# A three-stage decoder layer on one core: context loaded batch by batch, shorter lags, four load buffers, and routes moved beside the first group's spreading

## What is computed

```python
# layer 1: causal linear attention, one 16-wide head repeated 16 times
qkv = x @ qkv_w.T + qkv_b;  q, k, v = split(qkv, 3)
wei = where(tril, einsum('btd,bsd->bts', q, k), 0)
x = layernorm(x + tile(wei @ v, 16) @ proj_w.T + proj_b)
# layer 2: each batch's 77 ctx rows are aligned to its 256 x rows by dynamic time warping
D = sqrt(max(|ctx|^2 + |x|^2 - 2 ctx.x, 0))            # 77 x 256 per batch
R[i, j] = D[i, j] + min(R[i-1, j], R[i, j-1], R[i-1, j-1])
path = backtrack(R);  x = layernorm(x + sum of ctx rows along the path)
# layer 3: product-key memory with 64*64 experts, batch norm over all 8192 rows ahead of the query
xn = batchnorm(x) * gamma + beta;  q = (xn @ w_q.T)    # 2 halves, 8 heads, 128 wide
scores, idx = top_k(q . keys, 8)                       # per half
sc, pk = top_k(scores0[:, None] + scores1[None, :], 8) # 8 of the 64 sums
h = sigmoid(sc) * gelu(x . down[indices])
x = layernorm(x + sum of h * up[indices])
```

## Time and profile before

| | |
|---|---|
| time, median of 3 executions | 2913.73 us |
| lowest and highest | 2905.39 and 2916.35 us |
| the profiled execution: its own time | 2907.08 us |
| its span | 2905.3 us |
| mean granted PE clock | 0.956 |
| PE busy | 2652.9 us (91%) |
| DVE, POOL, ACT busy | 76%, 30%, 26% |
| stage 1, to the first DVE instruction of stage 2 | 207.4 us |
| recursion and path of stage 2 | 207.4 to 383.7 us |
| batch loop of stage 2 | 383.7 to about 480 us |
| stage 3 | from about 485 us to the end |

### The profile page before, as it was taken

The page is one execution under the profiler, slowest core; times in us unless marked ns, Lnnn a source line. Parts: engine busy times, 40 slices in busy tenths (PEclk is TensorE's granted clock), DMA queues, the critical chain, the costliest instruction groups (busy, mean ns, idle before and its releaser), DMA issues.

```text
span 2905.3 us, 104629 instructions
## 1 busy us (share of the span) xinstructions
PE 2652.9 (91%) x43108; PEld 2293.1 (79%) x43108; DVE 2210.9 (76%) x7510; ACT 761.9 (26%) x1340; POOL 857.1 (30%) x670
## 2 busy tenths in 40 slices
PE   6961167799999999999999999999999999999996
PEld 5851145688888888888888888888888888888895
DVE  5668966877777777777777777777777778777744
ACT  4740055322222222222222222222222222222210
POOL 1330142233333333333333333333333333333332
PEclk9985589999999999999999999999999999999997
DMA  5550337400000000000000000000000000000000
GB/s 174 172 161 23 65 112 177 72 13 13 11 13 10 13 12 12 13 13 13 14 13 13 13 14 13 13 14 13 13 14 13 13 13 14 13 14 13 10 10 12
DMA packets 84630, 99.34 MB, mean 34 GB/s; under 512 B 6189, under 2 KB 74702, under 8 KB 84046
## 3 DMA queue, kind: packets, MB, share of 16 engines
q1 hardware_dynamic: 84190, 92.94, 11.5%
HBM read 65.13 MB, written 27.79 MB: 32 GB/s over the span
## 4 chain that ended last, share of the span: by engine, by line
PE 82%; issue 7%; DVE 1%; DMA 1%; ACT 1%; POOL 0%; POOLq 0%; DVEq 0%; SPq 0%; ACTq 0%
PE bank L1078 32%; PE bank L1112 31%; PE bank L1096 9%; PE bank L1049 8%; PE bank L767 1%; DMA x_again<-x_scratch 1%; PE bank L770 1%; PE bank L1064 1%; PE bank L1036 1%; DVE hot L1295 0%; ACT x_sb L727 0%; POOL best L664 0%; DMA x_scratch<-x_sb 0%; DVE shared L1307 0%; ACT L1197 0%
## 5 line engine op out<-in xcount | busy, mean ns | idle before, releaser
L1015 POOL TENSOR_TENSOR hot<-hot,valsT 128x512 f32<-128x512 f32 x512 | 733.0, 1451 | 1662.8 <-DVE hot L1295 1662.8
L1078 PE MATMUL bank<-x2T,shared 128*64 128x128 f32 x16384 | 951.4, 274 | 4.6 <-issue 3.1
L1078 PEld LDWEIGHTS bank<-x2T,shared 128*64 128x64 f32 x16384 | 889.8, 137 | 26.6 <-issue 11.9
L1295 DVE TENSOR_TENSOR hot<-places,valsT 128x1024 f32<-128x1024 f32 x512 | 647.6, 1305 | 0.2 <-issue 0.2
L1112 PE MATMUL bank<-up,shared 64*128 64x256 f32 x4096 | 449.4, 379 | 1.5 <-DVE shared L1307 1.5
L1112 PE MATMUL bank<-up,gelh 64*128 64x256 f32 x4096 | 446.4, 377 | 0.0
L1112 PEld LDWEIGHTS bank<-up,shared 64*128 64x128 f32 x4096 | 397.1, 188 | 58.9 <-issue 11.4
L1112 PEld LDWEIGHTS bank<-up,gelh 64*128 64x128 f32 x4096 | 395.2, 187 | 56.2 <-issue 11.5
L1096 PE MATMUL bank<-hot 64*64 64x64 f32 x16384 | 303.1, 224 | 30.9 <-POOL hot L1015 16.3
L1096 PEld LDWEIGHTS bank<-hot 64*64 64x64 f32 x16384 | 267.9, 137 | 79.7 <-issue 79.7
L1307 DVE TENSOR_TENSOR shared<-bank,shared 128x512 f32<-128x512 f32 x256 | 164.7, 685 | 176.8 <-PE bank L1096 176.4
(11 more groups left out here) (151 smaller groups left out, 2169.5 us busy)
## 6 DMA issues: line engine op xcount, KB each, us to landing
x_scratch<-x_sb SPq DMA_DIRECT2D x64, 256.0 KB, 2.1
xT_sb<-in_xT SPq DMA_DIRECT2D x32, 256.0 KB, 2.9
x_sb<-in_x SPq DMA_DIRECT2D x32, 256.0 KB, 3.0
x_again<-x_scratch SPq DMA_DIRECT2D x32, 256.0 KB, 2.8
x_tile<-x_scratch SPq DMA_DIRECT2D x32, 256.0 KB, 3.9
up<-in_table SPq DMA_DIRECT2D x2, 4096.0 KB, 37.0
yo<-x_scratch SPq DMA_DIRECT2D x32, 256.0 KB, 3.0
out_y<-yo SPq DMA_DIRECT2D x32, 256.0 KB, 2.0
```

Of the source, the lines that this page charges most:

```text
L1015: pool.tensor_tensor(lo, lo, valsT[:, par, 2, TQ * q:TQ * (q + 1), None].to_broadcast([P, TQ, NK]), ALU.mult).then_inc(gated_ready, 1)
L1078: mm = pe.matmul(ps_h[q % 2][half(c), i, :], dnT[:, k, lo // 2, half(lo % 2)], x2T[:, par, k, c, :], start=(k == 0), stop=(k == CC - 1))
L1295: dve.tensor_tensor(hot[:, q % SLOTS], places[:, None, None, :].to_broadcast([P, 2, TQ, NK]), valsT[:, par, 0:2, TQ * q:TQ * (q + 1), None ...
```

## The change

1. **Stage 1.** ctx is loaded one batch at a time (`load_ctx`, two transfers of 77 KB), with two buffers for its columns; `norms` takes one batch per step with another instruction. All lags are shorter, and the order of the lists is another: `dist` runs 4 steps behind `qkv`, was 7. SP's list is written out in full: `load_x` lag 1, `store_x1` 5, `store_dist` 7, and a new `load_cost` at lag 8, which brings each batch's distances back as `cost` as soon as they are stored. The first x transfer goes ahead of the weights, a small Sqrt is done before anything waits, the reduction of the projection is cut in two, and the start of PE needs only some of POOL's constants (`pads`).
2. **Stage 2.** The `cost` loads are gone from its start. DVE's recursion waits only for the first of POOL's fills. `x1_again` has four buffers: `load(b)` waits for `warp(b-4)`, and the store is at lag 6, was 3.
3. **Stage 3.** DVE does `hots` of group 0 ahead of `route(1, 0)`, and `route(1, 1)` after the step of group 0, followed by `route(2, 0)`, `hots` of group 1 and `route(2, 1)`; so in that step no `hots` of group 1. PE turns the values of group 0 after `hidden` 6, was 8, and those of group 1 inside `output(0)`. ACT's gates move with them.

The diff, cut to its core:

```diff
-            ctx_cols = sa("ctx_cols", [P, CC, NB, S2])
+            ctx_cols = sa("ctx_cols", [P, CC, 2, S2])
...
+                def load_ctx(b, par):
+                    if later(b, 2):
+                        sp.wait_ge(norm_seen, b - 1)
+                        sp.wait_ge(ctxm2_ready, b - 1)
+                    sp.dma_start(ctx_rows[:, b, :], ctx_rows_d[b]).then_inc(rows_in[par], 16)
+                    sp.dma_start(ctx_cols[:, :, par, :], ctx_cols_d[:, b].rearrange("(k p) s -> p k s", k=CC))\
+                        .then_inc(cols_in[par], 16)
...
+                def load_cost(b, par):
+                    sp.wait_ge(dist_out[par], dmas(b, par))
+                    sp.dma_start(cost[b:P:NB, :], dist_d[b].rearrange("(g f) -> g f", g=NG)).then_inc(cost_in[par], 16)
...
-                pipeline(sp, [(load_xT, 0), (load_x, 5), (store_x1, 7), (store_dist, 10)], 12)
...
+                for i in range(1, NB + 9):
+                    for stage, lag, first in ((load_xT, 0, 2), (load_x, 1, 0), (store_x1, 5, 0), (store_dist, 7, 0),
+                                              (load_cost, 8, 0), (load_ctx, 4, 0)):
+                        if first <= i - lag < NB:
+                            stage(i - lag, (i - lag) % 2)
...
-                pipeline(pe, [(head, 2), (qkv, 0), (wei, 1), (turn_v, 1), (attn, 3), (turn_x1, 6), (dist, 7)], 10)
+                pe.wait_ge(pads, 1)
+                pe.wait_ge(w_in, 16 * 6)
+                pipeline(pe, [(qkv, 0), (head, 1), (dist, 4), (wei, 0), (turn_v, 0), (attn, 1), (turn_x1, 2)], 6)
...
-                pipeline(act, [(root, 9), (head, 2), (qkv, 0), (wei_off, 1), (ctx_scale, 6), (x1_cols, 6), (std, 4)], 12)
+                pipeline(act, [(qk, 0), (std, 2), (v, 0), (head, 1), (wei_off, 0), (ctx_scale, 3), (root, 4), (x1_cols, 2)], 6)
...
-                pipeline(dve, [(residual, 4), (recip, 5), (dist, 8), (wei_diag, 1), (v, 1), (setup, 1), (settle, None),
-                               (norms, 4), (stats, 4), (scale, 5), (settle, None), (aggr, 4)], 10)
+                pipeline(dve, [(recip, 2), (dist, 4), (settle, None), (scale, 2), (wei_diag, 0), (v, 0), (setup, 0),
+                               (residual, 1), (norms, 3), (settle, None), (stats, 1), (settle, None), (aggr, 1)], 6)
...
-            x1_sb = sw("x1_again", [P, 2, NT, C])
+            x1_sb = sw("x1_again", [P, 4, NT, C])
...
-                for g in range(NG):
-                    sp.dma_start(cost[NB * g:NB * (g + 1), :], dist_d[:, RG * T * g:RG * T * (g + 1)])\
-                        .then_inc(cost_in[g], 16)
...
-                pipeline(sp, [(load, 0), (store, 3)], 6)
+                pipeline(sp, [(load, 0, 4), (store, 6)], 8, unroll=4)
...
                     for lo in range(NK):
+                        if lo == 20 and not later(g, 1):
+                            turn_vals(1)
...
-                    if q == 8:
+                    if q == 6:
                         turn_vals(0)
...
-                route(1, 0)
                 for q in range(SLOTS):
                     hots(0, 0, q)
-                route(1, 1)
+                route(1, 0)
...
-                    if within(g, 2):
+                    if not later(g, 1):
+                        route(1, 1)
+                        route(2, 0)
+                        for q in range(SLOTS):
+                            hots(1, 1, q)
+                        route(2, 1)
+                    elif within(g, 2):
                         route(g + 2, 0)
                         route(g + 2, 1)
```

More of the change, by code:

```diff
@@ L81, in decoder_layer @@
         dn = shared[:, DN:].rearrange("p (j c) -> p j c", c=C)
+        cost = shared[:, 0:RG * T]
         w_in = sem("w_in")
         wq_in = sem("wq_in")
-        ctx_in = [sem(f"ctx_in{i}") for i in range(NB // 8)]
+        rows_in = [sem(f"rows_in{i}") for i in range(2)]
+        cols_in = [sem(f"cols_in{i}") for i in range(2)]
+        norm_seen = sem("norm_seen")
+        pads = sem("pads")
         consts = sem("consts")
@@ L118, in decoder_layer @@
         dist_out = [sem(f"dist_out{i}") for i in range(2)]
-        cost_in = [sem(f"cost_in{g}") for g in range(NG)]
+        cost_in = [sem(f"cost_in{i}") for i in range(2)]
         table_init = sem("table_init")
@@ L128, in decoder_layer @@
         bounds_ready = sem("bounds_ready")
-        x1_in = [sem(f"x1_in{i}") for i in range(2)]
+        x1_in = [sem(f"x1_in{i}") for i in range(4)]
         short_ready = sem("short_ready")
@@ L319, in _ @@
                 pool.memset(wqkv[:, :, GAP + HS:2 * GAP], 0.0)
+                pool.memset(proj[:, :], 0.0)
+                pool.memset(eps_col[:, :], EPS)
+                pool.drain()
+                pool.nop().then_inc(pads, 1)
                 pool.memset(ones[:, :], 1.0)
@@ L363, in turn_v @@
                     pe.wait_ge(vT_ready, b + 1)
+                    if not later(b, 1):
+                        pe.wait_ge(consts, 1)
                     if later(b, 1):
@@ L454, in ctx_scale @@
                 def ctx_scale(b, par):
-                    if not later(b, 1):
-                        for part in ctx_in:
-                            act.wait_ge(part, 32)
+                    act.wait_ge(cols_in[par], dmas(b, par))
                     if later(b, 2):
@@ L618, in one, with load @@
                     return ap[bass.ds(b, 1)].rearrange("a p t c -> (a p) t c")
-                def load(b, par):
-                    if later(b, 2):
-                        sp.wait_ge(warp_mm, b - 1)
-                    sp.dma_start(x1_sb[:, par], one(x1b, b)).then_inc(x1_in[par], 16)
+                def load(b, lane):
+                    if later(b, 4):
+                        sp.wait_ge(warp_mm, b - 3)
+                    sp.dma_start(x1_sb[:, lane], one(x1b, b)).then_inc(x1_in[lane], 16)
                 def store(b, par):
@@ L966, in vals_of @@
             def vals_of(g):
-                return ps_vals0 if isinstance(g, int) and g == 0 else ps_vals
+                return ps_vals0 if isinstance(g, int) and g < 2 else ps_vals
             def within(g, n):
@@ L1102, in output @@
                     pe.wait_ge(coef_ready, NA * (g + 1))
-                    if within(g, 1):
+                    if within(g, 1) and later(g, 1):
                         pe.wait_ge(valsT_ready, g + 2)
@@ L1133, in first @@
                         coefs(g, n)
-                        if n == 5 and within(g, 1):
-                            turn_vals(g + 1)
+                        if n == 5:
+                            if within(g, 1) and later(g, 1):
+                                turn_vals(g + 1)
                             if within(g, 2):
@@ L1349, in step @@
                                 hots(g, par, q)
-                            elif within(g, 1):
+                            elif within(g, 1) and later(g, 1):
                                 hots(g + 1, 1 - par, q - NQ)
-                    if within(g, 2):
+                    if not later(g, 1):
+                        route(1, 1)
[4 more added lines that the diff above has]
+                    elif within(g, 2):
                         route(g + 2, 0)
```

77 lines of the change are left out of this document (36 added, 41 removed).

## The result

| | before | changed |
|---|---|---|
| time, median of 16 executions each | 2906.82 us | 2914.02 us |
| span of the profiled execution | 2905.3 us | 2912.4 us |
| mean granted PE clock | 0.956 | 0.958 |
| first instruction of the recursion, on DVE | 207.38 us | 228.95 us |
| first turning on PE in stage 3 | 486.23 us | 501.09 us |

The ratio of changed to before is 1.0021, with a 95% interval from 1.0013 to 1.0028: 0.2% slower, so within 0.5%, where I forecast 0.5% less and a range that ended at 2912. (One of the 16 executions of the kernel before took 4055 us; the ratio leaves it out.) Stage 2 gained what was forecast and stage 3 two thirds of it. Stage 1, which was to be 3 us shorter, is 21.6 us longer.

The account below looks back on a forecast made before the run. PE was taken to bound stage 1's middle and stage 3, a DVE chain stage 2's recursion. Stages gave -3 - 6 - 6 = -15 us, from 2913.7 to 2898.7, 0.5% less; range for 8 in 10: 2878 to 2912.

Parts of the forecast that it names:

- Stage 1, start: Start of stage 1: ctx transfers leave the path; `residual(0)` at about 19, `residual(4)` at 38, 20 us ahead of before.
- Stage 1, middle: Middle of stage 1: a loop from `residual` through the distance store and `dist` back makes a batch 5.7 us, not 4.98.
- L: Landing time of the distance store that `dist` waits for in stage 1, taken as 2.3 us.
- The loops behind it: Other stage 1 loops claimed shorter: DVE's step about 4.3 us, ACT's 4.7, PE's 4.98.
- that rival: Stage 1 middle: the store lands fast, L 1.7, batch 5.1, middle 15 us shorter, 2884 us in all; 25%.
- Stage 1, end: From `residual(30)` to the recursion: 18.5 us instead of 23.5, 5 less.
- Stage 2: Recursion loop: with four buffers the x1 load waits go, 2.6 us a batch for 2.81; 6 us less (3 to 8).
- Stage 3: Start of stage 3: `coefs(0, 1)` starts 13.1 us earlier, new holes take some back; 6 us less (3 to 8).
- The holes: Three new PE waits in stage 3: 3.3 us, 3.5 us, and 1.7 us from group 0's norm delaying two `hots`.
- the rival: New waits eat the later gains: stage 2 gives nothing, stage 3 3 us as holes lower PE's clock; 2908 us; 20%.
- slower: the store queues: Stage 1, `dist`'s wait: small transfers keep the queues busy, L 3.5, batch 6.9, 2929 us; 8%.

Follow-up runs that it names:

- e11: Changed kernel with x1 store, distance store and ctx load lags one less, and SP issuing the distance store first in its step: 2881.77 us, ratio 0.9910 to before.
- e4: Changed kernel without cost loads in SP's loop; four 640 KB transfers at the end of stage 1 instead: 2923.68 us, ratio 1.0062 to before.
- e12: Changed kernel with the distance store and ctx load lags one less (6 and 3), x1 store still at lag 5: 2887.91 us, ratio 0.9930 to before.
- e1: Changed kernel with only the distance store one step earlier on SP (lag 6 for 7): 2908.46 us, ratio 1.0006 to before.
- e10: Changed kernel with x1 store, distance store and ctx load lags one less, and DVE's `dist` behind `scale`: 2876.66 us, ratio 0.9896 to before.

## Why the prediction was wrong, point by point

**Stage 1, start: right but for 2.4 us.** `residual(0)` was forecast at about 19 and came at 19.60; `residual(4)` at 38 came at 40.41. 17.6 us ahead of before, not 20.

**Stage 1, middle: the mechanism was right, one term was mis-sized, and this is the step that failed.** The loop was drawn as it runs. Its sum was 3.39 + L, and L was taken as 2.3: "1.6 for the store alone ... and 0.7 for two large transfers ahead". Measured in the step shown, L is 2.91, and 2.8 in the median. The rest is 3.57 for 3.39: `dist` to `scale` is 0.73, not 0.55, since 0.25 us of idle lie between them (the row of `scale`). The batch is 6.48 in that step and 6.39 in the mean (3.57 + 2.82), not 5.7. `residual(5)` came at 46.94 where 43.3 was forecast, 2.4 of these 3.6 us from the start, and the 25 batches after it at 6.38 add 17.1: together the 20.7 us by which `residual(30)` (206.50) missed 185.8.

What was wrong in the 2.3: I added a small queueing term to a landing. The runs show what a landing of 80 KB is in this queue: it comes 0.2 us behind that of the last transfer ahead, and takes 1.7 where those have landed early enough, as in the kernel before. Issued 0.92 behind a load that lands in 2.9 and 0.51 behind an x1 store that lands in 3.1, it takes 3.1 - 0.51 + 0.2 = 2.8. And the x1 store itself had gone from 2.1 to 3.1 where it stands 0.41 behind a load; with one more transfer ahead (e11) it takes 3.8.

The Trainium skill (DMA: Bandwidth & Descriptors, Queues, rings and completion order) has this as its rule: a semaphore increment lands only after the earlier writes of the same DMA engine. I cited it, but applied it to the x load alone, which gave a bound of 2.1; applied to the x1 store as well, with the 3.1 that this store has in the changed kernel, it gives 2.6. The runs agree with the rule: none of the 165 stores lands ahead of a transfer issued before it, L follows the ctx columns in e11, and in e4 taking away transfers issued behind the store leaves L alone.

**The loops behind it: missed.** "The other loops are shorter" rested on each engine's own instructions. I did not close the loops through the other two transfers. e12 shows the one through the x1 store (5.44 a batch, with the changed kernel's lag for that store), e1 the one through `ctx_scale`, `root` and the ctx load (5.5 us in the rows shown, 5.97 a batch in the mean, with the distance store at lag 6). Both are longer than PE's 4.98. So by e12 a fast distance store alone would not have brought the middle down to the 5.1 of that rival, to which I gave 25%, but to 5.4 at best.

**Stage 1, end: 4 us too low.** From `residual(30)` to the recursion 22.45 us pass, forecast 18.5, before 23.5. `root(31)` comes 15.4 after `residual(30)`, where my terms up to `root` give 13.1 to 13.5; from there to the recursion it is 7.1, where I had 5.2 to 5.7.

**Stage 2: right.** 2.60 us a batch as forecast, no wait for `x_again`, 6.7 us gained for 6. `norm` waited for the x2 store only twice, 0.8 us in all.

**Stage 3: right in its steps, 4.1 us for 6.** `coefs(0, 1)` 21.6 us after the first `hots`, to the digit. The holes were 3.43 (3.3), 2.19 (3.5), and the third (1.7) did not appear. But `hots` started at 539.33, 1.1 us later than the forecast 523.4 moved by the 14.9 us; 1.36 us of idle stand ahead of them for PE's turning and ACT's copy of the values. And each of the two holes cost about 1.5 us more by the clock, which I had listed only for the rival: the scores took 8.65 for 7.13 us, and `coefs(1, 1)` and the `hidden` behind it 6.4 for 4.9.

**The sum.** Forecast -3 - 6 - 6 = -15. Read: +21.6, -6.7, -4.1 = +10.8 on PE, of which 9.7 are left at the last `scale` and 7.1 in the span; the medians say 7 us and the ratio 6 (4 to 8). The forecast of 2898.7 had been added to a median of 3 executions, 2913.73, which the 16 put at 2906.82. So in absolute time it missed by 15 us, and the change itself by 22; from 2906.82 the range would have ended at 2905, and it is luck that the measured 2914 lies only 2 us above 2912.

The rival "slower: the store queues" had the place and the direction, at 8%, and its remark that nothing is won at L = 2.9 came true. Its reason did not: it put the slow landing down to the small transfers that keep the queues busy, and e4 and e11 show that L follows the order of issue and not the traffic. The 3.5 of the earlier trace rows, which it leaned on, is another thing: ahead of that store stands only an x1 store, 0.98 us earlier, as ahead of those that land in 1.7. What delayed it stays open.

## What to carry to other kernels

When a schedule is tightened on a queue with waits in it, list each transfer of the list and close its loop: what frees its issue, what is issued ahead, its landing, its reader, and back. Every loop must be shorter than the engine's own batch time, and taking the longest one away only shows the next; here the three lags gave 31 us together; the distance store's alone gave 6, the ctx load's alone nothing, and with the x1 store's put back 5 of the 31 were lost. For the landing of a small transfer that a wait depends on, do not take its median from a place where it was alone: take the landing of each one ahead, in the new order of issue, minus the time between the two issues; the longest of these and 0.2 us was the landing here. Or issue the small one where nothing ahead is still under way.

## What was not expected of the hardware

- The landing of the distance store depended on the transfers ahead in the queue (0.2 us behind the last of them) and hardly on traffic. L was 2.8 at 174 GB/s, 2.9 at 159, 2.9 at 212 and 3.0 at 223; and 2.0 at 213 GB/s with the store issued first.
- 77 KB of ctx columns (pieces of 308 bytes) took 3.9 us where 256 KB of x took 2.9. Without the cost load ahead (e4) they took 3.2. How much of it is the small pieces and how much the transfers ahead no run separates.
- At 221 GB/s, with the DMA engines busy 0.83 of the time, PE still ran without a gap (e10): the queue had the room, and what had cost time in the changed kernel were the moments of issue.
